# Interleaving the first half of an FFN's second product with its first product in TensorE's program order

## The reference

```python
xn = _layernorm(x)                                  # x: 4 x 4096 x 1024
x = x + attn(xn, Wk, Wv, Wo, gate, freqs) + ffn(xn, gate_w, w1, b1, w2, b2)
# attn: k = exp(1j*10*(xn@Wk)); v = xn@Wv; running sums over time of v*binder,
#       times a probe, / sqrt(t+1), for a position and an association part; @ Wo
# ffn (as reshaped, per token): 8 experts, all computed for all tokens
for e in range(8):
    h = gelu(x_flat @ w1[e] + b1[e])                # 1024 -> 4096
    y = h @ w2[e] + b2[e]                           # 4096 -> 1024
    out = out + where(expert_idx == e, expert_w, 0)[:, None] * y
```

## Time and profile before

| | us |
|---|---|
| two timed runs | 5798.25 and 6248.47 (median 6023.36) |
| the profiled execution's own time | 5770.01 |
| its span (core 4, the slowest) | 5768.5 |
| the eight cores' spans | 5722.2 to 5768.5 |

### The profile page before, as it was taken

The page is one execution under the profiler, slowest core; times in us unless marked ns, Lnnn a source line. Parts: engine busy times, 40 slices in busy tenths (PEclk is TensorE's granted clock), DMA queues, the critical chain, the costliest instruction groups (busy, mean ns, idle before and its releaser), DMA issues.

```text
span 5768.5 us, 52392 instructions; the slowest of 8 cores (5722.2 to 5768.5 us)
## 1 busy us (share of the span) xinstructions
PE 4142.0 (72%) x18224; PEld 1848.0 (32%) x18224; DVE 1430.2 (25%) x2651; ACT 1747.5 (30%) x2240; POOL 434.1 (8%) x727
## 2 busy tenths in 40 slices
PE   1022287778777777887788777967888887987782
PEld 0012133333333333333333333423333333333331
DVE  2133211222121222122212232133311223123231
ACT  0011133433333333333333342233322333233330
POOL 0000000000000000001000100010000100010000
PEclk9999998889989889998899889988999988998996
DMA  5957565445444444458554945575546744483333
GB/s 78 115 101 107 119 165 152 132 138 150 131 130 135 138 130 141 152 124 192 145 156 123 215 133 142 163 141 144 149 147 142 191 145 142 132 203 124 121 113 116
DMA packets 371633, 810.04 MB, mean 140 GB/s; under 512 B 71080, under 2 KB 246440, under 8 KB 337584
## 3 DMA queue, kind: packets, MB, share of 16 engines
q0 software_dynamic: 226624, 409.01, 32.7%
q1 hardware_dynamic: 144752, 397.69, 21.5%
HBM read 930.36 MB, written 157.29 MB: 189 GB/s over the span
## 4 chain that ended last, share of the span: by engine, by line
PE 57%; ACT 18%; DVE 10%; DMA 8%; issue 5%; DVEq 1%; ACTq 0%; SPq 0%; POOL 0%; POOLq 0%
PE f_y L985 26%; PE f_h L922 23%; ACT L116 8%; DMA w1ring<-w1c 4%; ACT f_h L116 3%; DMA ln_x<-xfh 2%; PE a_kv L640 2%; PE a_kv L635 2%; DVE accf L116 2%; ACT a_bnt L116 1%; DVE ln_stg L116 1%; ACT a_bnp L116 1%; DMA o_x<-xown 1%; DVE a_bph L116 1%; DVE a_bth L116 1%
## 5 line engine op out<-in xcount | busy, mean ns | idle before, releaser
L922 PE MATMUL f_h<-f_xn,w1ring 128*128 128x512 bf16 x8192 | 1960.2, 398 | 888.1 <-ACT f_h L116 769.4
L985 PE MATMUL f_y<-f_w,f_h 128*128 128x512 bf16 x8192 | 1784.7, 380 | 52.5 <-DVE accf L116 50.8
L116 ACT ACT_TABLE_LOAD x432 | 554.3, 1283 | 3031.5 <-PE f_h L922 1496.3
L922 PEld LDWEIGHTS f_h<-f_xn,w1ring 128*128 128x128 bf16 x8192 | 813.0, 102 | 2022.2 <-issue 1201.3
L985 PEld LDWEIGHTS f_y<-f_w,f_h 128*128 128x128 bf16 x8192 | 801.3, 98 | 1029.3 <-issue 71.8
L116 ACT ACTIVATE f_h<-f_h,b_s 128x512 bf16<-128x512 f32 x1024 | 703.7, 687 | 756.1 <-PE f_h L922 729.5
L116 DVE SCALAR_TENSOR_TENSOR accf<-f_y,se_tm,accf 128x512 bf16<-128x512 f32 x224 | 168.2, 751 | 1294.0 <-PE f_y L985 1273.5
L116 DVE TENSOR_SCALAR a_tA<-a_bnp 128x512 f32<-128x512 f32 x64 | 27.6, 431 | 1598.1 <-ACT a_bnt L116 1598.1
L854 POOL DMA_DIRECT2D f_w<-w2c x512 | 274.6, 546 | 1951.5 <-PE f_y L985 1796.0
L416 PE MATMUL ln_tr<-ident_s,ln_xn 128*128 128x128 f32 x256 | 62.1, 424 | 393.1 <-DVE ln_xn L116 393.1
L116 DVE TENSOR_TENSOR_SCAN a_cb<-a_p,carries,consts 128x512 f32<-128x512 f32 x256 | 328.6, 1283 | 27.6 <-DVE a_p L116 1.4
(11 more groups left out here) (69 smaller groups left out, 1428.4 us busy)
## 6 DMA issues: line engine op xcount, KB each, us to landing
f_w<-w2c POOLq DMA_DIRECT2D x512, 512.0 KB, 4.2
w1ring<-w1c SPq DMA_DIRECT2D x256, 1024.0 KB, 6.2
w1c<-w POOLq DMA_DIRECT2D x64, 1024.0 KB, 20.2
w2c<-w POOLq DMA_DIRECT2D x128, 512.0 KB, 10.0
f_xn<-xnscr SPq DMA_DIRECT2D x32, 1024.0 KB, 10.2
a_wk<-wkc SPq DMA_DIRECT2D x64, 256.0 KB, 6.1
a_wv<-wvc SPq DMA_DIRECT2D x64, 256.0 KB, 6.8
ln_x<-xfh SPq DMA_DIRECT2D x16, 512.0 KB, 5.5
```

Of the source, the lines that this page charges most:

```text
L116: ins = fn(*a, **k)
L922: ins = t.matmul(hps[ctg % NHPS][:, 0:FCH], w1ring[:, slot * KT * W1CO + kt * W1CO + ct * P: slot * KT * W1CO + kt * W1CO + (ct + 1) * P], ...
L985: ins = t.matmul(yps[tt][:, 0:MMW], hsb[:, kc * FCH + tt * P: kc * FCH + (tt + 1) * P], w2ring[:, slot * KCG * MMW + k2 * MMW: slot * KCG ...
```

## The change

The first half (hh = 0) of the second product is no longer emitted after all w1 blocks. Behind w1 block cob (for cob 2 to 7), after the attention tick and the cast, group cob - 2 of half 0 is emitted; groups 6 and 7 follow behind block 7's group 5. Then come the four drains of half 0, the loads of half 1's w2 pieces, tick 8, half 1 as before, its drains and tick 9. The body of a group and of the drains is moved into two functions and is otherwise the same.

```diff
+            def emit_f2_kcg(e, c, gi, hh, kcg):
+                up = (gi * NH + hh) * NKCG + kcg
+                ...
+                    wt.need(t, tok_g_w2p[up])
+                    wt.need(t, tok_s_h[(e, c, kcg * KCG + KCG - 1)])
+                    if kcg == 0 and uh >= 1:
+                        for tt in range(NTT):
+                            wt.need(t, tok_v_yev[(uh - 1, tt)])
+                    ... (16 matmuls, as before)
+            def emit_f2_evacs(e, c, gi, hh):
+                ... (4 drains, as before)
                     au_tick()
                     if cob in (0, 3, 6):
                         emit_cast_pieces(1)
-
-                for hh in range(NH):
-                    ... (8 groups in one block, then w2 loads, drains, au_tick)
+                    if 0 <= cob - 2 < NKCG:
+                        emit_f2_kcg(e, c, gi, 0, cob - 2)
+
+                for g_ in range(min(NKCG, max(0, NCOB - 2)), NKCG):
+                    emit_f2_kcg(e, c, gi, 0, g_)
+                emit_f2_evacs(e, c, gi, 0)
+                gpc[0] += NKCG
+                if NH > 1:
+                    emit_w2_pieces(e, 1, gpc[0])
+                    au_tick()
+                    for g_ in range(NKCG):
+                        emit_f2_kcg(e, c, gi, 1, g_)
+                    emit_f2_evacs(e, c, gi, 1)
                     gpc[0] += NKCG
+                au_tick()
```

More of the change, by code:

```diff
@@ L854, in _ @@
                             g.dma_start(dst, src))
+            def emit_f2_kcg(e, c, gi, hh, kcg):
+                up = (gi * NH + hh) * NKCG + kcg
+                uh = gi * NH + hh
+                slot = up % W2SLOTS
+                @block.tensor
+                def _(t, e=e, c=c, hh=hh, gi=gi, up=up, uh=uh, kcg=kcg,
+                      slot=slot):
+                    wt.need(t, tok_g_w2p[up])
[3 more added lines that the diff above has]
+                            wt.need(t, tok_v_yev[(uh - 1, tt)])
+                    ins = None
+                    for tt in range(NTT):
+                        for k2 in range(KCG):
+                            kc = kcg * KCG + k2
+                            ins = t.matmul(
+                                yps[tt][:, 0:MMW],
+                                hsb[:, kc * FCH + tt * P:
+                                    kc * FCH + (tt + 1) * P],
+                                w2ring[:, slot * KCG * MMW + k2 * MMW:
+                                       slot * KCG * MMW + (k2 + 1) * MMW],
+                                start=(kcg == 0 and k2 == 0),
+                                stop=(kcg == NKCG - 1 and k2 == KCG - 1))
+                        if kcg == NKCG - 1:
+                            tok_t_f2stop[(uh, tt)] = T.inc(ins)
+                    tok_t_w2free[up] = T.inc(ins)
+                    if hh == NH - 1:
+                        tok_t_hsbfree[(gi, kcg)] = tok_t_w2free[up]
@@ new lines, in emit_f2_evacs, with _ @@
+            def emit_f2_evacs(e, c, gi, hh):
+                uh = gi * NH + hh
+                for tt in range(NTT):
+                    ttg = c * NTT + tt
+                    @block.vector
+                    def _(v, e=e, c=c, tt=tt, ttg=ttg, hh=hh, uh=uh):
+                        v = AE_V(v)
+                        wvv.need(v, tok_t_f2stop[(uh, tt)])
+                        dst = accf[:, ttg * DM + hh * MMW:
+                                   ttg * DM + (hh + 1) * MMW]
+                        if e == 0:
+                            v.tensor_scalar(
+                                dst, yps[tt][:, 0:MMW],
+                                se_tm[:, ttg * NE + e:ttg * NE + e + 1],
+                                None, ALU.mult)
+                        else:
+                            v.scalar_tensor_tensor(
+                                dst, yps[tt][:, 0:MMW],
+                                se_tm[:, ttg * NE + e:ttg * NE + e + 1],
+                                dst, ALU.mult, ALU.add)
+                        tok_v_yev[(uh, tt)] = V.tok
+                        if e == 0:
+                            tok_v_acc[(0, c, tt)] = V.tok
@@ L965, in build_program @@
                         emit_cast_pieces(1)
-                for hh in range(NH):
[L968 to L999, removed]
-                    gpc[0] += NKCG
[L1001 to L1028, removed]
```

## The result

| | before | after |
|---|---|---|
| ratio, after to before | | 1.016, 95% interval 1.0138 to 1.0183 |
| timed runs, us | 5779 to 5798 | 5871 to 5897 |
| the profiled execution's span, slowest core, us | 5768.5 (core 4) | 5877.6 (core 6) |
| spans of cores 3 and 6, us | 5767.3, 5755.9 | 5860.4, 5877.6 |

The changed kernel is 1.6% slower, some 93 us: slower as forecast, but by less than the forecast 2.2%. In some executions of either kernel one die or both were granted a lower clock and took longer; the times and ratios in this document leave such executions out, and the readings of traces such cores.

A forecast was written before the change was run, and what follows sets the result against it. TensorE's waits in the 32 FFN passes, mostly on gelus, were taken to bound the kernel. Terms -103.5 + 129 + 5 + 135 - 45 + 8 = +128.5 us on 5770 gave 5900 us (ratio 1.022), range 5810 to 6040.

The forecast's parts named there:

- slow restarts: TensorE's matmuls at the lower clock behind new long waits, at tick 7 and expert boundaries: 2 us each.
- (1): Gelu waits behind attention tiles at ticks 2 to 6: each 3.45 us shorter by one moved group, -103.5 us.
- (2): Half 0's drains wait behind VectorE's work on seven tiles at tick 7: +129 us; two tiles at tick 6: +5.
- (3): Heads of passes 12, 16, 20, 24, 28: w2 pieces late for group 0 behind forced casts on POOL, +135 us.
- (5): Half 1's w2 pieces, issued in one burst behind block 6's cast, land late: +8 us, bounds 0 and 40.
- (4): Each w1 load from block 2 on has 3.45 us more, so w1 waits shrink: -45 us, bounds 0 and -60.
- faster, by the clock: Rival: 10.2 us gelu waits no longer lower TensorE's clock, saving 31 restarts (62 us): 5685 us; chance 0.05.
- Casts arrive in time: Rival: casts speed up once w1 loads stop, expert boundaries cost 60 us or less: 5820 us; chance 0.14.
- Heavier: Rival: no relief for boundary casts, half-1 pieces late in most passes, smaller w1 gain: 6010 us; chance 0.18.
- nothing: Rival: gains and losses cancel, the filled waits reopening elsewhere: 5770 us; chance 0.03.

The follow-up runs named there:

- e3: The changed kernel with six casts a pass (behind blocks 0 to 5) and tick 7's attention unit behind half 0's drains: ratio 0.9626 to the kernel before.
- f1: The kernel before, its order of blocks and halves kept, with attention tiles only at ticks 7 and 8 of a pass: ratio 0.8937.
- f4: Kernel before with tiles at ticks 7/8, six casts a pass, block 7 split around groups 0 to 4; then K/V weight loads earlier, three casts in half 1: ratio 0.8511.

## Why the prediction was right or wrong, point by point

The direction, both new waits, their places and their number came out as written. What failed is the size of the sum: +128.5 us was written, and the timed runs grew by 93, so that the larger chance (0.55 for more than 2% slower, against 0.40 for less) was misplaced. The steps that failed are two terms of the sum. The slow restarts were put at +16 us, eight new ones, and the time outside the waits did not grow at all: -7.6 us on core 6, -4.2 on core 3. And the gain on w1 loads was put at -45, where core 3 showed -60.4. On core 3, which grew by 93.1 us as the timed runs did, these two make up 35.6 us, and the other rows of the table cancel to within 1 us of the forecast.

- **(1) Filled waits, -103.5, with the 13.6 of pass 12 about -117.** Measured -111.8 on core 6 and -109.4 on core 3. Right in mechanism, since most such waits are 10.15 to 10.52 us. The forecast 650 us was 14 us low.
- **(2) Tick 7, +121 of waiting; tick 6, +5.** Measured +124.9 on core 6 and +124.3 on core 3, with waits of 18.95 us and up to 26.3 against the written 18.9 and 26.3. This was read from two instruction dates of before and the order of one queue, and was the surest term.
- **(3) Expert boundaries, +135 net, or 141 of waiting on f_w.** Core 6: 148.4 us in the five long waits. With the short waits of (5), the longer cores of the four pairs had 141.5 to 154.6 in all, and the forecast for both was 149. The shorter ones had 85.1 to 114.6, or 102.6 to 114.6 with waits at passes 16 and 20 that the profile books on operations of the tile. The size is right partly by luck, since two errors cancel. The relief was put at 11 us a boundary, 55 in all. On core 6, from the first forced cast to the first piece load, the five boundaries took 333.1 us before and 306.9 after: 26 us in all, 16 of them in pass 28. And I read the dates on core 4, where they gave 182 us; the same reading of core 6 before gives some 17 us less.
- **(4) w1 loads, -45, bounds 0 and -60.** Core 6 -45.0, core 3 -60.4. The first load cannot be held fixed at 35.0: it was 25.2 to 35.0 in the eight cores before and 23.0 to 35.8 after. Without it the waits went from 70.1 to 17.2 us on core 6 and from 73.5 to 13.8 on core 3, that is by 53 and 60. The walk through the waits had given 53, and the 8 us that I took off for new contention had no row behind them.
- **(5) Half-1 pieces, +8.** In the trace of core 6 two waits beyond the long five, 6.2 us together. Right.
- **Slow restarts, +16.** The lower level did come after 10.16 us; the "faster, by the clock" rival falls. But I counted only the restarts that the change adds and not those that go with the w1 waits. Core 6 before:

```profile
1846.22 5.34 PE L922 MATMUL f_h<-f_xn,w1ring 128*128 128x512 bf16 x16 [6.74 <-DMA w1ring<-w1c]
```

These 16 matmuls take 5.34 us instead of 3.62. Added up on core 3 over all waits above 1.2 us, what the matmuls behind them took beyond 0.2155 us each went from 6 to 30 us behind the waits of the second product, from 27 to 6 behind w1 waits and from 119 to 107 behind gelu waits.
- **From the sum to the ratio.** The absolute forecast, 5900 us, lies near the measured 5871 to 5897 partly by luck: it was added to a profiled 5770, and the timed runs of before that it is to be compared with took 5779 to 5798.
- **The rivals.** "Casts arrive in time" (term (3) at 60 or less) came true on no core, the shorter ones of the pairs included. "Heavier" and "nothing" did not occur.

The Trainium skill's rule that I set beside (3) (DMA: Bandwidth & Descriptors, Queues, rings and completion order: each DMA engine takes turns, packet by packet, between queue rows that have work) would have casts go faster once the w1 queue is empty. The trace of core 6 agrees in direction, with 26 us over five boundaries instead of 55; no run here separates this rule from whatever sets the two cores of a pair apart.

## What to carry to other kernels

A wait that one moved group of matmuls shortens by 3.45 us may be covered whole by placing its cause elsewhere: moving 64 attention tiles to the two places that have 27.6 us of independent work behind them was worth 10.6%, where filling the waits was worth at most 3.7% (e3). When work is moved forward, list for each queue what it is moved past and what it now wants early (here a drain behind a tile on VectorE, eight loads behind twelve casts on POOL, two loads behind a 1 MB one on SP). When an added wait brings a slow restart, count also the restarts of the waits that go. And before a core's trace is laid beside its own in another execution, look at whether it was the longer of its pair in both.

## What the runs showed of the hardware

- The two cores of a pair take unlike times for the same casts, and which is the slower changes from execution to execution. In the changed kernel's profiled execution the longer core of each pair waited 141.5 to 154.6 us on f_w, the shorter one 85.1 to 114.6 (with up to 17.5 booked elsewhere). What sets them apart stays open.
- A piece load of 512 KB lands in 4.2 us (median), but in 57 us when three casts stand before it in POOL's queue (f1).
- The granted clock stands at 0.50 behind a wait of 10.16 us as behind one of 13.97, and the restart costs about the same (5.18 us for 16 matmuls instead of 3.62, and 8.59 for 32 instead of 7.07). It comes behind shorter waits too: 5.34 us for 16 matmuls behind 6.74. In f4, without long waits, the mean granted clock of the cores is 0.983 to 0.987, against 0.920 to 0.923 before.
- ScalarE loads its table anew at the head of a block's gelus even where gelus ran just before, and it does so after the matmuls that it waits for:

```profile
2890.58 0.69 ACT L116 ACTIVATE f_h<-f_h,b_s 128x512 bf16<-128x512 f32 x1 [1.04 <-PE f_h L922]
2892.29 1.28 ACT L116 ACT_TABLE_LOAD   x1 [1.02 <-PE f_h L922]
2893.58 1.47 ACT L116 ACTIVATE f_h<-f_h,b_s 128x512 bf16<-128x512 f32 x2
```

These 1.28 us stand before the gelu that the third column tile waits 0.54 us for. Such waits are what is left of the gelu waits in f4 (118.5 us, none above 0.8); a kernel without the reload was not run.
